# Keeping a comparison's number ramp in PSUM beside a matmul's sum: a two-layer graph network on one Trainium2 core

## The reference

```
x_src = h[src];  x_dst = h[dst];  e = edge_emb[edge_type]        # 16 edge types
messages    = ((x_src + e) @ msg_W + msg_b) * (1 + 0.5*tanh(gamma)) + beta
edge_delta  = tanh(gelu(concat(x_src, x_dst, e, task) @ att_W1 + att_b1) @ att_W2 + att_b2)
edge_weight = 1 + edge_scale * edge_delta
agg = segment_sum(messages * edge_weight, dst);  deg = segment_sum(edge_weight, dst)
agg = agg / max(deg, 1) ...  then a node update, a residual and a layer norm
```

## Time and profile before

| | us |
|---|---|
| median of 3 runs | 1418.08 |
| lowest and highest run | 1410.15, 1423.96 |
| the profiled execution | 1410.3 |
| its span, first to last instruction | 1408.5 |
| mean granted TensorE clock | 0.812 |

### The profile page before, as it was taken

The page is one execution under the profiler, slowest core; times in us unless marked ns, Lnnn a source line. Parts: engine busy times, 40 slices in busy tenths (PEclk is TensorE's granted clock), DMA queues, the critical chain, the costliest instruction groups (busy, mean ns, idle before and its releaser), DMA issues. The chain is left out here.

```text
span 1408.5 us, 18435 instructions
## 1 busy us (share of the span) xinstructions
PE 915.3 (65%) x4908; PEld 707.3 (50%) x4908; DVE 904.7 (64%) x2667; ACT 614.6 (44%) x1493; POOL 933.6 (66%) x892
## 2 busy tenths in 40 slices
PE   5502223331133410499979999989999999998795
PEld 4402122321123400277757777667677777776464
DVE  5476575655566544367557877777777767777357
ACT  5433333333234323123246655556565555555333
POOL 3477777777777777472357777777777777776012
PEclk9855555665555555699989999999999999999798
DMA  5487666656866565346556777777777777778402
GB/s 151 118 187 262 214 194 209 215 193 215 269 215 213 196 216 197 126 135 165 155 158 192 216 212 222 209 212 215 210 220 214 215 214 210 215 214 182 102 21 72
DMA packets 105123, 266.58 MB, mean 189 GB/s; under 512 B 25099, under 2 KB 45712, under 8 KB 98880
## 3 DMA queue, kind: packets, MB, share of 16 engines
q0 software_dynamic: 54560, 166.61, 41.0%
q1 hardware_dynamic: 48672, 97.03, 21.4%
q10 hardware_dynamic: 1792, 1.75, 0.5%
HBM read 195.82 MB, written 68.81 MB: 188 GB/s over the span
## 5 line engine op out<-in xcount | busy, mean ns | idle before, releaser
L681 POOL DMA_INDIRECT gath<-hp_d,chain_src x391 | 388.8, 994 | 131.9 <-issue 120.3
L1337 POOL DMA_INDIRECT gbuf<-pm_d,srcs x357 | 385.6, 1080 | 121.9 <-issue 105.2
L918 DVE SCALAR_TENSOR_TENSOR hist<-hist,smask,gath 128x256 f32<-128x256 f32 x390 | 189.1, 485 | 210.0 <-ACT gath L714 201.9
L714 ACT ACTIVATE gath<-gath,chain_w 128x256 f32<-128x256 f32 x391 | 167.3, 496 | 338.6 <-DMA gath<-hp_d,chain_src 338.6
L1447 PE MATMUL ps<-qw,halves 128*128 x1275 | 213.5, 276 | 40.9 <-DMA gbuf<-pm_d,srcs 27.2
L1665 DVE TENSOR_TENSOR acc<-ps,acc 112x272 f32 x425 | 186.9, 440 | 78.9 <-DVE acc L1665 49.1
L1449 PE MATMUL ps<-gbuf,ident 128*128 128x256 f32 x714 | 215.6, 384 | 0.0
L1521 ACT ACTIVATE gbuf<-ps 128x512 f32<-128x512 f32 x180 | 107.5, 598 | 199.4 <-PE ps L1449 199.2
L836 PE MATMUL ps<-win_hot,node_hot 128*112 128x28 bf16 x391 | 42.3, 247 | 233.7 <-DVE win_hot L1017 233.7
L1447 PEld LDWEIGHTS ps<-qw,halves 128*128 128x128 bf16 x1275 | 125.6, 99 | 124.0 <-issue 58.7
L1468 PE MATMUL ps<-gbuf,placed 128*112 128x272 f32 x714 | 178.7, 393 | 1.0 <-ACT placed L1542 1.0
(11 more groups left out here) (281 smaller groups left out, 1357.8 us busy)
## 6 DMA issues: line engine op xcount, KB each, us to landing
hist_d<-hist SPq DMA_DIRECT2D x48, 1024.0 KB, 4.6
gath<-hp_d,chain_src POOLq DMA_INDIRECT x391, 3.0
wn<-node_row_d SPq DMA_DIRECT2D x27, 224.0 KB, 3.7
key<-node_row_d SPq DMA_DIRECT2D x26, 224.0 KB, 3.6
gbuf<-pm_d,srcs POOLq DMA_INDIRECT x357, 4.0
pm_d<-gbuf SPq DMA_DIRECT2D x6, 896.0 KB, 5.1
hp_d<-hpo SPq DMA_DIRECT2D x7, 448.0 KB, 3.2
hb_d<-gbuf SPq DMA_DIRECT2D x7, 448.0 KB, 3.3
```

The source lines that it names most:

```text
L681: eng.indirect_dma_start(row_at(j), None, hp_d[:, :], bass.IndirectOffsetOnAxis(ap=chain_src[:, j:j + 1], axis=0)).then_inc(got[q % RINGG] ...
L714: eng.activation(row_at(j), row_at(j), ACT.Copy, scale=chain_w[:, j:j + 1]).then_inc(gw_ready, 1)
L918: eng.scalar_tensor_tensor(out=state_at(j), in0=state_at(j - 1) if j else first_state[:, :], scalar=smask[:, j:j + 1], in1=row_at(j), op0= ...
L1337: eng.indirect_dma_start(gath3(g % RING)[:, k, 0:2 * D], None, pm_d[:, :], bass.IndirectOffsetOnAxis(ap=srcs[:, g * SG + k:g * SG + k + 1] ...
```

## The change

A ramp of 128 numbers and one column with the partition's number are copied from SBUF (`iof`, `pcol`) into bank 7 of PSUM, right of the 272 columns of the fourth slot sum, once ahead of the edge stage. The three comparisons of a group read the ramp or the number there. `match_keys`, until now a `tensor_scalar` with a per-partition scalar, becomes a `tensor_tensor` whose second input is the number repeated 512 times. Since PE writes the fourth slot sum into the same bank, PE waits ahead of that matmul until DVE has made the comparisons of the group (`match_ready`) and the key comparison of the next (`hot_ready`). Ahead of the two copies DVE waits until the last users of bank 7 are done (`pm_v`, `pm_a`).

```diff
+            ramp = bank(7)[:, AW:AW + P]
+            pnum = bank(7)[:, AW + P:AW + P + 1]
...
+            ramp_set = sem("ramp_set")
...
                         for k in range(slots_in(g - 2)):
                             wait(eng, summed, (g - 3) * SG + k + 1)
+                            if k == SG - 1:
+                                eng.wait_ge(match_ready, min(g + 1, NGR))
+                                eng.wait_ge(hot_ready, min(g + 2, NGR))
                             eng.matmul(bank(4 + k)[0:WIN, 0:AW], place[q % 3][:, k * WIN:(k + 1) * WIN],
...
-                    eng.tensor_scalar(hot[g % 2], key[n % 2][:, at:at + GW], pcol[:, 0:1], None, ALU.is_equal).then_inc(hot_ready, 1)
+                    eng.tensor_tensor(hot[g % 2], key[n % 2][:, at:at + GW], pnum.to_broadcast([P, GW]), ALU.is_equal).then_inc(hot_ready, 1)
+                eng.wait_ge(pm_v, 2 * NG)
+                eng.wait_ge(pm_a, 2 * NG)
+                eng.tensor_copy(ramp, iof[:, :]).then_inc(ramp_set, 1)
+                eng.tensor_copy(pnum, pcol[:, 0:1]).then_inc(ramp_set, 1)
+                eng.wait_ge(ramp_set, 2)
                 match_keys(0)
...
-                        eng.tensor_tensor(gath3(r)[:, :, 2 * D:SW], bc(iof[:, 0:TY], SG), bi(edgef[:, e0:e0 + SG], TY), ALU.is_equal)
-                        eng.tensor_tensor(place[r % 3][:, :].rearrange("p (k t) -> p k t", k=SG), bc(iof[:, 0:WIN], SG),
+                        eng.tensor_tensor(gath3(r)[:, :, 2 * D:SW], bc(ramp[:, 0:TY], SG), bi(edgef[:, e0:e0 + SG], TY), ALU.is_equal)
+                        eng.tensor_tensor(place[r % 3][:, :].rearrange("p (k t) -> p k t", k=SG), bc(ramp[:, 0:WIN], SG),
```

## The result

| | before | after |
|---|---|---|
| median of the runs, us | 1415.74 (4 runs, 1410.15 to 1423.96) | **1372.69** (4 runs, 1371.06 to 1374.49) |
| ratio | | 0.9716, 95% interval 0.9676 to 0.9756 |
| profiled execution, us | 1410.3 | 1371.06 |
| its span, us | 1408.5 | 1369.3 |

The kernel is faster by 43 us. The span lost 39.2 us, and the trace says where. In what follows the lines of the kernel after are: gather L1340, z L1450 and L1452, slot sums L1474, key comparison L1661, the two comparisons with the ramp L1679 and L1680, logits L1689.

The account below looks back on a forecast made before the run. PE nearly bounds the edge stage, held up by POOL's late gathers: 44.1 us lost, less 7.0 and 3 kept, gives 34, less 1 for entry, 33. Profiled 1410.3 to 1377.3 us; median 1418.1 to 1385, range 1368 to 1409.

Parts of the forecast that it names:

- What bounds the kernel, and what is late next: Edge stage: PE nearly the bound but kept waiting by POOL's late gathers; PE's own 523.8 us of work comes next.
- Two rivals: Edge stage: DVE becomes the bound (12%, 1404 us), or the DMA transfers bind (13%, 1401 us).
- What stretches POOL: POOL's gather issues: the one-input key comparison was said to cause 48.4 of 56.8 us excess, the ramp comparisons none.
- The rival of 7%: POOL's long issues have another cause than the key comparison and stay: 1418 us, chance 7%.
- The key at 0.68 us: DVE's key comparison with a PSUM input: from 0.345 to 0.68 us, at most 1.083.
- DVE's 36 us more work: DVE over 107 groups: the slower key comparison adds 36 us of work, hidden behind PE.
- The ramp comparisons: DVE's two comparisons reading the ramp in PSUM: no gain, each longer by 0 to 0.01 us.
- Has DVE room: DVE's chain per step: 4.95 us plus 0.01, recovered in pair steps; 34.7 against PE's 35.7 us over seven steps.
- PE's new wait at no cost: PE ahead of the fourth slot sum: slack 1.06 us, cost 0, up to 0.3 us after a late Gelu.
- Entry: Ahead of the first key comparison: two copies, one semaphore wait and the longer key cost 1 us in all, once.
- The slower rival: PE stops ahead of the fourth slot sum: key of 0.98 us gives back all, 1.08 means 1432 us; 6%.
- The size: Edge stage: 34 us gained of 44.1, keeping 7.0 for waits at its end and 3 for other late landings.

Follow-up runs that it names:

- e8: Against the kernel after: the third bf16 part of `qw` left out of z, so PE has less work; 1363.92 us, ratio 0.9658 to the kernel before.
- e11: Against the kernel after: key comparison back to the one-input SBUF form, ramp comparisons still reading PSUM; 1370.97 us, ratio 0.9698 to the kernel before.
- e10: Against the kernel after: an extra 192-column `tensor_tensor` with both inputs in SBUF ahead of each key comparison; 1538.24 us, ratio 1.0054 to the kernel before.
- e5: Against the kernel after: the old one-input key comparison added as an extra ahead of each key comparison; 1387.11 us, ratio 0.981 to the kernel before.
- e1: Against the kernel after: ramp comparisons read SBUF again, only the key comparison reads PSUM; 1544.6 us, ratio 0.9975 to the kernel before.
- e7: Against the kernel after: the key comparison made twice, the first into an unread tile; 1421.01 us, ratio 1.0042 to the kernel before.
- e6: Against the kernel after: an extra 192-column `tensor_tensor` with one PSUM input ahead of each key comparison; 1390.0 us, ratio 0.983 to the kernel before.
- e3: Against the kernel before: the key comparison made a `tensor_tensor` with both inputs in SBUF; 1568.88 us, ratio 1.0145.
- e2: Against the kernel after: key comparison back to the one-input SBUF form, ramp still in PSUM; 1543.59 us, ratio 0.999 to the kernel before.
- e9: Repeat of e2, the ramp alone in PSUM, against the kernel after; 1524.75 us, ratio 1.0003 to the kernel before.
- e4: Against the kernel before: only PE's two new waits ahead of the fourth slot sum added; 1543.91 us, ratio 0.9982.

## Why the prediction was right, and where it was wrong

*What bounds the kernel, and what is late next: right.* PE's need of 523.8 us from z of group 3 to 106 was to be the floor, and 527.1 was measured. e8 shows the floor from the other side: with less work for PE the time falls, until DVE binds. POOL was given 507 us and took 504. Two rivals are settled by the same rows. DVE didn't become the bound: its waits for Gelu shrank from 61.6 to 9.3 us. The transfers didn't bind: their share rose to 0.79, as reckoned (0.78), and 2.8 us of waits for gathers are left.

*What stretches POOL: this step failed.* I gave the 48.4 us of excess to the key comparison and said of the ramp that "nothing is gained there". It is the reverse: 36.5 us came in by the ramp comparisons, 11.0 by the key, and e11 has the whole gain without touching the key. The mistake lies in the sorting. I sorted issues by what they **overlap**, and found 103 beside L1655 at 1.417 us and 42 beside L1668 or L1669 alone at 0.948. But L1655 follows L1669 with no gap, so an issue that L1669 holds lasts long enough to reach L1655 and is counted there; what is left beside L1669 alone are the issues that were not held. The outcome had picked the class. Sorted by what runs when they begin, the same rows tell the opposite, and the earlier trace rows had it: 744.66 begins beside L1655, but the 1.78 us of 1164.73 begins 0.88 us ahead of L1655 and ends 0.82 us behind L1669.

I leaned on the Trainium skill, "SBUF — State Buffer", section "Who interferes with whom". It says that a `tensor_tensor` takes only the read side of the ports shared with GpSimd, and infers that the writing of descriptors isn't held by it. The same section says that a DVE instruction with two SBUF inputs contends with a GpSimd instruction that reads SBUF, and the prediction passed over that. These gathers take their row numbers from `srcs`, a tile in SBUF, so the section gave grounds to suspect L1668 and L1669 too. The measurement decides for the suspicion: a `tensor_tensor` with both inputs in SBUF holds an issue just as long as the one-input form of equal length, 1.12 us in e10 and 1.11 in e5. Whether the issue is held in reading or in writing, no run here separates. What the section says of the one-input form stands, and so does its remark that whichever comes first blocks the other: beside an issue under way the one-input key was stretched from 0.344 to as much as 0.569 us in e11.

The forecast survived by luck: both kinds of comparison were changed at once, and the sum that goes away, 46 us measured (56.8 to 10.7), hardly depends on which of them gets the blame. Had only the key been changed, as the prediction's account would have allowed, most long issues would have stayed (e1). The rival of 7% had its condition half met, as the long issues had mostly another cause than L1655, but the change took that cause away as well.

*The key at 0.68 us:* 0.676. *DVE's 36 us more work:* 35 by the durations, but its busy time in the stage rose by only 24 us (426 to 450), as neighbouring instructions overlap. *The ramp comparisons:* 0.614 instead of 0.617 us, within the bound for their length. *Has DVE room:* yes. *PE's new wait at no cost:* no such wait is in the list of the stage; e7 shows when it costs. *Entry:* 1 us was set aside; the copies and the longer key stand ahead of the first z, which begins at 728.17 where it began at 728.26. PE's wait ahead of it grew from 7.70 to 8.12 us, so at most 0.4 us can be laid to it.

*The slower rival:* its place was right, its price too high. It let a key of 0.98 us give back the whole gain. e5 and e6 add an instruction of 0.35 us to the 0.68 (0.27 from start to start) and give back 14 to 17 of 43 us; e7 adds 0.68, and only that gives back all. In e7 the step behind each pair still takes 4.88 us and the next 5.2 to 5.4: the slack of the step with a pair takes up more of DVE's lag than I had allowed.

*The size:* the gain in the stage was 40.8 instead of 34 us. I had kept 7.0 us of waits at the end of the stage and 3 for other late landings; 3.3 were left of all. Those gathers were late because the lead was spent, not because transfers bound: in the stage after, the transfers carry more, 226 against 209 GB/s. Against it stand the 2.6 us of a lower clock in the last layer, which the prediction had at nothing ("only moves forward") and which may be chance. 1377.3 was forecast for the profiled execution, and 1371.06 came. The median lies 12.3 us below the forecast, 6.2 by that and the rest because the profiled run of before lay 7.8 us under its median and that of after 1.6.

## What to carry to other kernels

To find what holds an engine up, sort its instructions by what runs elsewhere when they **begin**, and never by overlap: a held instruction overlaps whatever comes next, and the one that follows the culprit gets the blame. Then look where the held ones end: here 0.82 us behind one particular instruction, which names it. Where GpSimd issues indirect gathers one after another and DVE works beside it, move one operand of DVE's longest comparison to PSUM first: here that cost nothing in length, and took away most of what POOL lost. It brought 43 us where POOL's issues set the pace, and nothing on the chips where they didn't. Making a short one-input operation slower to the same end wasn't needed.

## What the runs showed of the hardware

- A gather's issue on POOL that begins while DVE runs an instruction with all inputs in SBUF (two inputs, or one in the fast one-input form) ends 0.82 us behind the end of that instruction or of the run that it begins: 1.12, 1.41, 1.44, 1.78 and 2.39 us in the rows above, where 0.947 is usual. With one input in PSUM it isn't held at all (0.947 over 99 issues).
- An issue that is already under way is not held in e10 (0.95 from 0.05 us on). In the kernel before, however, 17 issues that began 0.2 us ahead of L1668 took 1.77 us. Which moment decides is open. The hold passes on to an instruction with two SBUF inputs that follows (L1668 to L1669, L1669 to the two-input key in e3, the key to the first logit), and not from L1669 to the one-input key of before; why is open too.
- The one-input comparison of 512 bf16 columns takes 0.344 us, and up to 0.57 where it begins 0.49 to 0.69 us into an issue that isn't held: then it ends 1.06 us behind the start of the issue (16 times in e11, 37 in e2); its two-input twin of 0.347 us in e10 never exceeds 0.357.
- The same kernel takes 1414 us on some chips and 1525 to 1548 on others, and on the latter shorter issues bring nothing (e2, e9). Between 850 and 1200 us the DMA share is 0.67 in e4, the kernel before with two waits more, on such a chip, against 0.73 in the kernel before.
